# RWKV of batch 0 and the state-space constants placed in the last attention's final slots, late weights loaded there

## The chip, the cores and the metric

The kernel runs on one NeuronCore of a Trainium2 chip. The metric is the device time in microseconds (us) of the whole program, the median of several runs. Engines are called by their names in the profile: PE (TensorE), ACT (ScalarE), DVE (VectorE), POOL (GpSimd), SP (SyncE, which only issues DMAs here). Each has an instruction stream of its own, executed in order; they meet at semaphores.

## The reference, cut to what matters

The input is x, 8 batches of 512 tokens by 128 channels. Eight residual steps follow, each of the form x + layer(layernorm(x)):

```python
x = x + _L2_attn_ref(_layernorm(x), W_qkv)              # full attention, 16 heads of 8
x = x + _L2_ffn_ref(_layernorm(x), W_r, W_k, W_v, mu_r, mu_k)
x = x + _L3_attn_ref(_layernorm(x), W_in, conv_w, conv_b, W_x, B_log, W_out, ln_g, ln_b)
x = x + _L3_ffn_ref(_layernorm(x), ...)                 # experts

# _L2_ffn_ref, the RWKV channel mix
xr = mu_r * x + (1.0 - mu_r) * x_prev
xk = mu_k * x + (1.0 - mu_k) * x_prev
r = sigmoid(xr @ W_r.T)
out = r * (square(relu(xk @ W_k.T)) @ W_v.T)
```

The four steps before these are a block-masked attention, an FP4 FFN, an ALiBi attention and a ternary FFN. `_L3_attn_ref` is a state-space layer: projection, short convolution, silu, a scan with decay 0.95, a product with C times exp(B_log), a gate, an output projection and a layernorm of its own. The product of W_x's C part with exp(B_log) doesn't depend on x; it is one 256x256 matrix, `couple`.

## The kernel before, in words

X stays in SBUF throughout, 128 partitions by 8 x 512 columns, one 512-column stretch per batch. There are six stages: attention, FP4 FFN, attention, ternary FFN, attention (`l2`, kind "full"), and `Tail`, which runs the RWKV layer (`RwkvFfn`), the state-space layer (`Ssm`) and the experts (`ExpertFfn`) as a pipeline of batches. A stage starts on each engine with `stage_starts`: wait until the stage before has written X of batch 7 (`s_x_done`).

**The attention's order.** `frames` runs a body for c from -1 to 8, and each frame has 16 slots (`slots`). In frame c the slots 0 to 7 hold key groups 8 to 15 of batch c-1, the slots 8 to 15 groups 0 to 7 of batch c; the row maxima of the next batch are computed beside them. In the last frame (c = 8) only groups 8 to 15 of batch 7 are left, in slots 0 to 7, and no maxima. A slot on PE: two score heads (`head_t`, L398 or L386 in the trace), half of the previous group's product with V (`half_pv`, L412, 8 matmuls), two more heads, the other half. ACT does four `exp` per slot (L593). PSUM banks 0 to 2 hold scores, 3 to 5 the scores for the maxima, 6 the product with V, 7 the rest. After each quarter ACT copies bank 6 (L606), PE transposes it (`context_t`, through `transpose4`, L2878), DVE divides it (L749, L751), and after the fourth quarter POOL adds it to X (L899). The attention takes a `guest`: after every slot each engine calls the guest's `early_*`. In this kernel only the first attention has one (the FP4 stage).

**The normalised batch 0 of the tail** is made in the attention's frame 7 already (`norm_stats`, `norm_apply` for batch `c + 1 = 8`, which `norm_of` turns into batch 0 of the next stage).

**The tail's order.** `Tail.frames` runs c from -3 to 7. Frame c works on the experts of batch c, opens the experts of c+1, runs the state-space layer of c+2 and RWKV of c+3. So frame -3 has nothing but RWKV of batch 0, and at its end (`opening`) the state-space constants: `exp(B_log)` on ACT (L1855), the product on PE (L1814), its copy into `couple` (L1857). Frame -2 begins on PE with the transposes of the state-space layer's batch 0 (`Ssm.pe_turn`) and holds the folding of the expert weights (`folding`).

RWKV of one batch: turn (PE, L2878), two scaled copies (ACT, L1709), mix (DVE, L1731), keys (PE, L1688), relu (ACT, L1714), square (POOL, L1742), receptance (PE, L1693), sigmoid (ACT, L1719), values (PE, L1701), product (DVE, L1737), add to X (POOL, L1747). Then comes the state-space norm: statistics (DVE, L1626, L1631), `Norm.apply` (POOL, L1638 to L1647) and `pool_shift` (POOL, L1945).

**The late weights** are 27 transfers (`load_late`, L2807), issued by SP at the stage's start, because they go into `Qst`, `V` and `Kst`, which the attention uses until its end. The first 8 of them are the state-space layer's and count on `s_late`, the other 19 on `s_later`. POOL waits at the start of its tail stream for all 19 (`e.k.wait_late(pool)`), ahead of `pool_square`.

`Qst`, `V` and `Kst` have a half for even and one for odd batches.

Of the kernel before, what the change touches and what calls it, by code (L numbers as in the profile page):

```python
# [20 lines left out]
NB = 8  # L21
# [1630 lines left out]
class RwkvFfn:  # L1652

    def __init__(self, k, st, bank, tile):
        def s(name, per):
            return k.started(f"rwkv_{name}", per)

        self.k, self.bank = k, bank  # L1660
# [73 lines left out]
    def dve_product(self, dve, n):  # L1734
        dve.wait_ge(self.s_v_ps.sem, self.s_v_ps.at(n))
        dve.wait_ge(self.s_x_done.sem, self.s_x_done.at(n.plus(-1)))
        dve.tensor_tensor(self.prod, self.bank, self.r, ALU.mult).then_inc(self.s_prod.sem, 1)  # L1737
# [5 lines left out]

    def pool_add(self, pool, n):
        pool.wait_ge(self.s_prod.sem, self.s_prod.at(n))
        x = xs_of(self.k.X, n)
        pool.tensor_tensor(x, x, self.prod, ALU.add).then_inc(self.s_x_done.sem, 1)  # L1747


class Ssm:  # L1750
# [6 lines left out]
    def __init__(self, k, before, banks, old, tile):  # L1757
# [36 lines left out]
        self.loads = len(k.late_loads)  # L1794
        self.expb = k.late([self.STATE, self.D_IN])
        self.couple = k.late([P, self.MT, self.D_IN])
        self.decay = k.sb("decay", [P, 1])
# [11 lines left out]

    def pe_constants(self, pe):  # L1810
        self.loaded(pe)
        pe.wait_ge(self.s_expb, 1)
        for kt in range(self.MT):
            mm = pe.matmul(self.banks[0][:, self.D_IN * kt:self.D_IN * (kt + 1)], self.wx[:, P * kt:P * kt + P],  # L1814
                           self.expb[:, :], start=True, stop=True)
        mm.then_inc(self.s_couple_ps, 1)
        pe.wait_ge(self.s_couple, 1)

# [33 lines left out]

    def act_constants(self, act):
        self.loaded(act)
        act.activation(self.expb[:, :], self.blog[:, :], ACT.Exp).then_inc(self.s_expb, 1)  # L1855
        act.wait_ge(self.s_couple_ps, 1)
        act.activation(self.couple[:, :, :].rearrange("p a b -> p (a b)"), self.banks[0], ACT.Copy)\  # L1857
           .then_inc(self.s_couple, 1)
# [26 lines left out]

    def dve_stats(self, dve, n):
        dve.wait_ge(self.before.sem, self.before.at(n))
        self.norm.stats(dve, n)
# [404 lines left out]
class Tail(Stage):  # L2293
# [5 lines left out]

    def __init__(self, k, stage, fp4, ternary):  # L2300
        self.fp4, self.ternary = fp4, ternary
        super().__init__(k, stage)

    def prepare(self, k):
# [6 lines left out]
        ps = [k.ps[:, j, :] for j in range(8)]  # L2311
        self.rwkv = RwkvFfn(k, self, ps[5], tile)
        self.ssm = Ssm(k, self.s_x_done, ps[6:8], self.fp4.q_x, tile)
# [3 lines left out]
    def frames(self, body):  # L2317
        for c in range(-3, NB):
            body(N(None, c), c == -3, c == -2)

    def tensor(self, pe):
# [3 lines left out]

        def frame(f, opening, folding):
            before, en, sn, rn = f.plus(-1), f.plus(1), f.plus(2), f.plus(3)
            for j in range(e.STEPS):
# [52 lines left out]
                elif j == 7:  # L2381
                    if sn.valid():
                        s.pe_out(pe, sn)
            if opening:
                s.pe_constants(pe)

        self.frames(frame)
        end = N(None, NB - 1)
# [4 lines left out]
    def scalar(self, act):  # L2393
        self.k.stage_starts(act, self)
        r, s, e = self.rwkv, self.ssm, self.expert

        def frame(f, opening, folding):
            before, en, sn, rn = f.plus(-1), f.plus(1), f.plus(2), f.plus(3)
            for j in range(e.STEPS):
# [40 lines left out]
                elif j == 7:  # L2440
                    if en.valid():
                        e.act_exp(act, en)
            if opening:
                s.act_constants(act)

# [3 lines left out]
    def vector(self, dve):  # L2449
        self.k.stage_starts(dve, self)  # L2450
        r, s, e = self.rwkv, self.ssm, self.expert
        r.dve_constants(dve)
        s.dve_constants(dve)

        def frame(f, opening, folding):
            before, en, sn, rn = f.plus(-1), f.plus(1), f.plus(2), f.plus(3)
            for j in range(e.STEPS):
# [53 lines left out]
    def gpsimd(self, pool):  # L2511
        self.k.stage_starts(pool, self)
        r, s, e = self.rwkv, self.ssm, self.expert
        e.k.wait_late(pool)

        def frame(f, opening, folding):
            en, sn, rn = f.plus(1), f.plus(2), f.plus(3)
# [6 lines left out]
            if rn.valid():  # L2524
                r.pool_add(pool, rn)
# [56 lines left out]
def make_stages(k):  # L2582
# [13 lines left out]
    fp4, ternary = Fp4Ffn(k, 1), TernaryFfn(k, 3)  # L2596
    fp4.after, ternary.after = l1, l2
    l0.guest, fp4.before = fp4, l0
    return [l0, fp4, l1, ternary, l2, Tail(k, 5, fp4, ternary)]

# [76 lines left out]
class Kernel:  # L2677


    def __init__(self, nc, ctx, dram, out):  # L2680
# [63 lines left out]

        self.late_mem = [self.Qst[:, :, :, :].rearrange("p a h t -> p (a h t)").bitcast(F32),
                         self.V[:, :, :, :, :].rearrange("p a t h e -> p (a t h e)"),
                         self.Kst[:, :, :, :].rearrange("p a h t -> p (a h t)").bitcast(F32)]
        self.late_at = [0, 0, 0]
        self.s_late = self.sem("late_weights")
# [30 lines left out]
    def late(self, shape, src=None, dt=F32):  # L2780

        size = int(np.prod(shape[1:])) * mybir.dt.size(dt) // 4
        r = next(r for r in range(3) if self.late_at[r] + size <= self.late_mem[r].shape[1])
        at = self.late_at[r]
# [171 lines left out]
def transformer(nc, dram, out):  # L2956
    with ExitStack() as ctx:
# [7 lines left out]
        def _(sp):  # L2965
# [76 lines left out]
```

## Time and profile before

| | us |
|---|---|
| median of 3 runs | 2067.47 |
| lowest, highest | 2064.45, 2068.32 |
| the profiled execution | 2065.46 |
| its span, first to last instruction | 2063.6 |
| PE busy | 1811.4 (88%) |
| DVE busy | 1298.7 (63%) |
| ACT busy | 1043.0 (51%) |
| POOL busy | 709.3 (34%) |

Times in the rows are us from the span's start. The last attention runs from about 1288 to 1654, the tail from there to the end. Only the join of the two is touched. A row of a timeline gives start, length, engine, line, operation, the tiles written and read, and how many instructions are merged; the bracket behind it is the engine's idle time before it and what ended that. PE's ends are modelled, and neighbours overlap: the distance of two starts tells more than the length.

### The profile page before, as it was taken

The page shows a single profiled execution, that of the slowest core. Times are in us where ns is not written, and L with a number is a line of the kernel's source. Part 1 is how long each engine was busy: PE and PEld are TensorE (multiplying, and loading weights), DVE is VectorE, ACT ScalarE, POOL GpSimd, SP SyncE. Part 2 cuts the span into 40 slices and gives each one's busy share as a digit, 9 for nine tenths or more (in the row PEclk, how much of TensorE's full clock was granted, in tenths as well). Part 3 has the DMA queues.
Part 4 walks back from the last instruction along what each step waited for, and adds up shares of the span by engine and source line. Part 5 has one row for each costly group of instructions (what it writes and reads, how often), then busy time and mean ns, then how long its engine had stood idle before and what let it go on. Part 6 is the DMA issues. An engine that isn't in the chain of part 4 may idle for free.

```text
span 2063.6 us, 33125 instructions
## 1 busy us (share of the span) xinstructions
PE 1811.4 (88%) x11885; PEld 815.9 (40%) x11885; DVE 1298.7 (63%) x3442; ACT 1043.0 (51%) x1768; POOL 709.3 (34%) x796
## 2 busy tenths in 40 slices
PE   4898888667669999988999999999999958999998
PEld 1233333234434444444445443333223234444443
DVE  3777777469867877761101114999899546666663
ACT  1566666522216666653322321888888834444432
POOL 4376676545522233201111102222223036444420
PEclk9899999777859999998999997999999978999999
DMA  6354222000033224400000020333222010000000
GB/s 132 98 140 95 63 63 63 1 17 1 0 101 85 63 63 103 84 2 3 0 0 1 0 57 6 98 81 70 63 63 63 2 51 1 6 6 6 6 11 11
DMA packets 67963, 91.68 MB, mean 44 GB/s; under 512 B 10924, under 2 KB 61340, under 8 KB 62924
## 3 DMA queue, kind: packets, MB, share of 16 engines
q1 hardware_dynamic: 66072, 89.04, 18.0%
q8 instruction: 95, 1.56, 0.3%
q10 hardware_dynamic: 1728, 0.53, 0.2%
q14 instruction: 68, 0.56, 0.1%
HBM read 49.30 MB, written 39.85 MB: 43 GB/s over the span
## 4 chain that ended last, share of the span: by engine, by line
PE 55%; issue 6%; DVE 4%; ACT 4%; DMA 2%; SPq 1%; POOL 1%; DVEq 0%; ACTq 0%; POOLq 0%
PE ps L1435 5%; PE ps L412 5%; PE ps L1447 5%; PE ps L2878 4%; PE ps L386 3%; PE ps L1412 3%; PE ps L370 3%; PE ps L2148 3%; PE ps L398 3%; PE ps L2150 2%; PE ps L2166 2%; PE ps L354 2%; PE ps L332 2%; DMA Qst<-mT 2%; ACT Pr L593 2%
## 5 line engine op out<-in xcount | busy, mean ns | idle before, releaser
L702 DVE TENSOR_REDUCE mx<-ps 128x1 f32<-128x512 f32 (+3 forms) x1024 | 534.3, 583 | 111.1 <-PE ps L354 82.6
L600 ACT ACTIVATE Pr<-ps 128x1024 f32<-128x1024 f32 (+3 forms) x512 | 348.0, 707 | 184.7 <-PE ps L337 95.9
L593 ACT ACTIVATE Pr<-ps 128x512 f32<-128x512 f32 x512 | 275.4, 601 | 44.9 <-PE ps L386 38.1
L354 PE MATMUL ps<-Kst,Qst 63*128 63x512 bf16 (+3 forms) x1024 | 223.2, 317 | 57.3 <-DVE mx L702 29.2
L698 DVE CUSTOM_DVE_ANT_0 vs<-ps,cT 128x512 f32<-128x512 f32 (+3 forms) x512 | 225.9, 488 | 63.2 <-PE ps L354 59.9
L332 PE MATMUL ps<-Qst,Kst 64*128 64x512 bf16 (+3 forms) x1024 | 223.4, 312 | 20.0 <-ACT Pr L600 8.3
L2906 POOL TENSOR_TENSOR ve<-mv,eps 128x4 f32<-128x4 f32 x41 | 8.3, 201 | 591.6 <-DVE mv L2895 591.6
L370 PE MATMUL ps<-Pr,V 128*32 128x512 f32 (+3 forms) x2048 | 198.4, 460 | 6.4 <-ACT ctxU L606 2.9
L398 PE MATMUL ps<-Kst,Qst 63*128 63x512 bf16 x512 | 172.5, 403 | 5.5 <-DVE mx L702 3.3
L412 PE MATMUL ps<-Pr,V 128*32 128x256 f32 x2048 | 164.6, 394 | 8.6 <-ACT ctxU L606 7.7
L386 PE MATMUL ps<-Qst,Kst 64*128 64x512 bf16 x512 | 157.2, 387 | 10.1 <-DMA Qst<-mT 5.8
L354 PEld LDWEIGHTS ps<-Kst,Qst 63*128 63x128 bf16 x1024 | 68.9, 95 | 194.4 <-DVE mx L702 99.4
L332 PEld LDWEIGHTS ps<-Qst,Kst 64*128 64x128 bf16 x1024 | 71.7, 94 | 121.2 <-ACT Pr L600 64.1
L1447 PE MATMUL ps<-f_shared,w_L_h2T 128*128 128x512 f32 x256 | 115.1, 592 | 0.0
L1435 PE MATMUL ps<-f_shared,w_L_h1T 128*128 128x512 f32 x256 | 112.8, 593 | 0.7 <-ACT xT L1523 0.7
L1580 DVE SCALAR_TENSOR_TENSOR f_shared<-ps,w_L_s_w,f_own 128x512 f32<-128x512 f32 x32 | 24.0, 750 | 122.6 <-PE ps L1412 118.1
L1562 DVE TENSOR_TENSOR ctxU<-ps,w_L_s_w 128x512 f32<-128x512 f32 x8 | 5.5, 692 | 151.4 <-PE ps L1424 151.4
L848 POOL TENSOR_TENSOR rec<-dn,mone 128x16 f32<-128x16 f32 x32 | 93.0, 2907 | 0.0
L337 PE MATMUL ps<-tri_kq,ident_h 64*128 64x128 bf16 x512 | 85.2, 220 | 0.0
L335 PE MATMUL ps<-tri_kq,ident_h 64*128 64x128 bf16 x512 | 85.1, 220 | 0.0
L412 PEld LDWEIGHTS ps<-Pr,V 128*32 128x32 f32 x2048 | 40.7, 108 | 95.6 <-issue 73.3
L386 PEld LDWEIGHTS ps<-Qst,Kst 64*128 64x128 bf16 x512 | 32.9, 94 | 113.5 <-ACT Pr L593 75.9
(340 smaller groups left out, 3277.9 us busy)
## 6 DMA issues: line engine op xcount, KB each, us to landing
Qst<-parts_scratch SPq DMA_DIRECT2D x48, 384.0 KB, 6.3
Kst<-parts_scratch SPq DMA_DIRECT2D x48, 384.0 KB, 8.4
parts_scratch<-qpart SPq DMA_DIRECT2D x24, 384.0 KB, 2.7
parts_scratch<-kpart SPq DMA_DIRECT2D x24, 384.0 KB, 3.3
parts_scratch<-qpart SPq DMA_DIRECT2D x24, 256.0 KB, 2.9
parts_scratch<-kpart SPq DMA_DIRECT2D x24, 256.0 KB, 3.3
parts_scratch<-qpart SPq DMA_DIRECT2D x24, 128.0 KB, 2.8
parts_scratch<-kpart SPq DMA_DIRECT2D x24, 128.0 KB, 3.3
```

Of the source, the lines that this page charges most:

```text
L332: mm = pe.matmul(out, k.Kst[rows, b.par, 2 * q + tile, P * jt:P * jt + P], k.Qst[rows, b.par, 2 * q + tile, T - W:T], start=True, stop=not ...
L354: mm = pe.matmul(ps[:, 4 + a, lo:lo + W], k.Qst[rows, n.par, pair, P * it:P * it + P], k.Kst[rows, n.par, pair, 0:W], start=True, stop=True)
L370: mm = pe.matmul(ps[32 * a:32 * a + 32, 6, lo:hi], k.V[:, b.par, jt, 4 * q + a, :], k.Pr[:, g % 2, a, lo - (T - W):hi - (T - W)], start=jt ...
L386: pe.matmul(ps[:, self.bank_t(b, g, j), :], k.Kst[rows, b.par, 2 * q + tile, P * jt:P * jt + P], k.Qst[rows, b.par, 2 * q + tile, :], star ...
L398: pe.matmul(ps[:, self.bank_m(n, u), :], k.Qst[rows, n.par, pair, P * it:P * it + P], k.Kst[rows, n.par, pair, :], start=True, stop=True). ...
L412: mm = pe.matmul(ps[32 * a:32 * a + 32, 6, lo:hi], k.V[:, b.par, jt, 4 * q + a, :], k.Pr[:, g % 2, a, lo:hi], start=jt == 0 and half == 0, ...
L593: act.activation(k.Pr[:, g % 2, 2 * (j // 2) + 1 - j % 2, :], ps[:, self.bank_t(b, g, j), :], ACT.Exp).then_inc(self.s_exp.sem, 1)
L600: act.activation(k.Pr[:, g % 2, 2 * tile:2 * tile + 2, 0:W], ps[:, 2 * tile:2 * tile + 2, 0:W], ACT.Exp).then_inc(self.s_exp.sem, 1)
L698: dve.tensor_tensor_reduce(k.vs[:, at_u % 2, T - W:T], ps[:, bank, lo:lo + W], k.cT[:, 1, T - W:T], 1.0, -3e38, ALU.add, ALU.max, k.mx[:, ...
L702: dve.tensor_reduce(k.mx[:, half, at:at + 1], ps[:, bank, lo:lo + W], AX_X, ALU.max, negate=True).then_inc(self.s_max.sem, 1)
L1435: mm = pe.matmul(ps[:, at + m, :], self.h1[:, kt, P * m:P * m + P], self.hidden[0][:, kt, :], start=kt == 0, stop=kt == self.KT - 1)
L1447: mm = pe.matmul(ps[:, at + m, :], self.h2[:, kt, P * m:P * m + P], self.hidden[1][:, kt, :], start=kt == 0, stop=kt == self.KT - 1)
```

## The change

`Tail` becomes the guest of the last attention, and its frame -3 is gone. What frame -3 did is spread over the attention's last frame (c = 8), behind the given slots: turn and the two scaled copies behind slot 0, mix behind 1, keys and relu behind 2, receptance behind 3, the gate r behind 4, values and product behind 6, the constants' `exp` behind 6, their product on PE behind 7 and its copy behind 8. The gate is no longer ACT's sigmoid: ACT does `exp(-x)`, DVE adds 1 and takes the reciprocal. POOL does `Norm.apply` of batch 1, square, add, `Norm.apply` of the state-space layer and `pool_shift`, all ahead of its last `X + ctx`. DVE does the statistics for the state-space norm of batch 0 ahead of the division of the last quarter.

The late weights all go to the even halves of `Qst`, `V` and `Kst`, which no batch uses after batch 6, and SP issues them after its last attention transfer, once batch 6 is done. Work areas of the experts go to the odd halves first; `expb` and `couple` move into `qpart`. POOL's wait for the 19 transfers moves behind the work of frame -2.

```diff
     def frames(self, body):
-        for c in range(-3, NB):
-            body(N(None, c), c == -3, c == -2)
+        for c in range(-2, NB):
+            body(N(None, c), c == -2)
+    def early_tensor(self, pe, f, s):
+        if f.c != NB:
+            return
+        r, zero = self.rwkv, N(None, 0)
+        if s == 0:
+            pe.wait_ge(self.before.s_max.sem, self.before.s_max.at(f.plus(-1)))
+            r.pe_turn(pe, zero)
+        elif s == 2:
+            r.pe_keys(pe, zero)
+        elif s == 3:
+            r.pe_receptance(pe, zero)
+        elif s == 6:
+            r.pe_values(pe, zero)
+        elif s == 7:
+            self.ssm.pe_constants(pe, self.k.ps[:, 4, :])
+
+    def early_scalar(self, act, f, s):
...
+        if s == 0:
+            r.act_first(act, zero)
+        elif s == 2:
+            r.act_relu(act, zero)
+        elif s == 4:
+            r.act_exponential(act, zero)
+        elif s == 6:
+            act.wait_ge(self.before.s_q_out.sem, self.before.s_q_out.at(f.plus(-1)))
+            self.ssm.act_exponential(act)
+        elif s == 8:
+            self.ssm.act_couple(act, self.k.ps[:, 4, :])
+
+    def early_vector(self, dve, f, s):
...
+        if s == 0:
+            r.dve_constants(dve)
+            self.ssm.dve_constants(dve)
+            r.norm.stats(dve, one)
+        elif s == 1:
+            r.dve_mix(dve, zero)
+        elif s == 4:
+            r.dve_inverse(dve, zero)
+        elif s == 6:
+            r.dve_product(dve, zero)
+        elif s == 8:
+            self.ssm.dve_stats(dve, zero, r.s_added)
+
+    def early_gpsimd(self, pool, f, point):
...
+        if point == 0:
+            r.norm.apply(pool, N(None, 1), r.s_xnT_ps)
+        elif point == 1:
+            r.pool_square(pool, zero)
+        elif point == 2:
+            r.pool_add(pool, zero, r.s_added)
+        elif point == 3:
+            ssm.norm.apply(pool, zero, ssm.s_res)
+            ssm.loaded(pool)
+            ssm.pool_shift(pool, zero)
...
+    def act_exponential(self, act, n):
+        act.wait_ge(self.s_r_ps.sem, self.s_r_ps.at(n))
+        act.activation(self.r, self.bank, ACT.Exp, scale=-1.0).then_inc(self.s_denominator.sem, 1)
+
+    def dve_inverse(self, dve, n):
+        dve.wait_ge(self.s_denominator.sem, self.s_denominator.at(n, 1))
+        dve.tensor_scalar(self.r, self.r, 1.0, None, ALU.add).then_inc(self.s_denominator.sem, 1)
+        dve.wait_ge(self.s_denominator.sem, self.s_denominator.at(n, 2))
+        dve.reciprocal(self.r, self.r).then_inc(self.s_r.sem, 1)
...
-        e.k.wait_late(pool)
-
-        def frame(f, opening, folding):
+        pool.memset(e.k.mone[:, :], -1.0).then_inc(r.s_x_done.sem, 1)
+
+        def frame(f, folding):
...
             if en.valid():
+                if en.c == 0:
+                    e.k.wait_late(pool)
                 e.pool_centre(pool, en)
...
                 if st.stage == max(FIRST_STAGE, FIRST_LATE):
-                    k.stage_starts(sp, st)
+                    attention, n = st.before, N(None, NB - 2)
+                    sp.wait_ge(attention.s_scores.sem, attention.s_scores.at(n))
+                    sp.wait_ge(attention.s_scores_t.sem, attention.s_scores_t.at(n))
+                    sp.wait_ge(attention.s_pv.sem, attention.s_pv.at(n))
                     k.load_late(sp, st.ssm.loads)
```

## Rows read from the trace of the kernel before

**Rows 1.** Windows: us, then each engine's busy us (and instructions), PE clock, DMA

```profile
1620.00:1640.00 20.00, 18.46 (x179) 5.98 (x176) 6.52 (x14) 17.83 (x37) 0.00 (x0) 1.00 0.01 1
1660.00:1680.00 20.00, 6.12 (x20) 4.73 (x20) 3.08 (x17) 4.48 (x6) 8.40 (x10) 0.50 0.34 97
```

**Rows 2.** The chain that ended last, at the join: start, us, what

```profile
1652.62 1.27 POOL X L899
1653.90 0.36 SPq L2807
...
1667.32 2.52 DMA V<-in_c_select
1670.05 1.05 POOL f_shared L1742
...
1680.34 1.94 PE ps L2878 x8
```

**Rows 3.** Timeline of SP's queue: its last transfers of the attention

```profile
1607.28 21.80 SPq L946 DMA_DIRECT2D Qst<-mT  x4
```

**Rows 4.** Timeline of PE: a part of a slot of the last frame, its end

```profile
1635.39 0.39 PE L386 MATMUL ps<-Qst,Kst 64*128 64x512 bf16 x2
1635.71 0.64 PE L412 MATMUL ps<-Pr,V 128*32 128x256 f32 x8
1636.28 0.57 PE L386 MATMUL ps<-Qst,Kst 64*128 64x512 bf16 x2
...
1649.41 1.07 PE L412 MATMUL ps<-Pr,V 128*32 128x256 f32 x16 [0.60 <-ACT Pr L593]
1651.29 0.63 PE L2878 MATMUL ps<-ident,ctxU 128*128 128x128 f32 x4 [0.81 <-ACT ctxU L606]
```

**Rows 5.** Timeline of ACT: last frame, then frame -3 of the tail

```profile
1632.66 0.63 ACT L606 ACTIVATE ctxU<-ps 128x512 f32<-128x512 f32 x1
...
1635.81 6.33 ACT L593 ACTIVATE Pr<-ps 128x512 f32<-128x512 f32 x12 [0.39 <-PE ps L386]
...
1655.35 0.68 ACT L1709 ACTIVATE f_shared<-ps,w_L_mu_k 128x512 f32<-128x512 f32 x1
1659.70 0.60 ACT L1714 ACTIVATE f_shared<-ps 128x512 f32<-128x512 f32 x1 [3.67 <-PE ps L1688]
1660.32 1.28 ACT L1719 ACT_TABLE_LOAD   x1
...
1664.37 0.42 ACT L1855 ACTIVATE Qst<-Qst 16x256 f32<-16x256 f32 x1
```

**Rows 6.** Timeline of PE: constants of frame -3, keys and receptance of frame -2

```profile
1673.21 2.07 PE L1814 MATMUL ps<-Qst 16*128 16x256 f32 x4
...
1686.67 1.02 PE L1688 MATMUL ps<-f_shared,w_L_WkfT 128*128 128x512 f32 x2
...
1689.69 1.05 PE L1693 MATMUL ps<-w_L_WrT,f_shared 128*128 128x128 f32 x8
```

**Rows 7.** DVE groups by shape: count, busy us, mean ns, idle before

```profile
L1023 DVE RECIPROCAL fq_h_inv<-fq_h_over 128x88 f32<-128x88 f32 x8 | 5.6, 703 | 0.3
...
L1028 DVE TENSOR_SCALAR f_shared<-f_shared 128x512 f32<-128x512 f32 x8 | 3.5, 440 | 0.3
...
L1023 DVE RECIPROCAL fq_x_inv<-fq_x_over 128x32 f32<-128x32 f32 x8 | 2.8, 353 | 0.3
```

**Rows 8.** Timeline of DVE: mix, product and statistics in frame -3

```profile
1656.13 1.41 DVE L1731 SCALAR_TENSOR_TENSOR f_shared<-ps,one_minus_mu,f_shared 128x511 f32<-128x511 f32 x2 [0.80 <-ACT f_shared L1709]
1673.32 0.69 DVE L1737 TENSOR_TENSOR f_shared<-ps,f_shared 128x512 f32<-128x512 f32 x1 [15.78 <-PE ps L1701]
1675.59 0.87 DVE L1626 BATCH_NORM_STATS2 ssm_bn<-X 128x6 f32<-128x128 f32 x4 [1.58 <-POOL X L1747]
```

**Rows 9.** Timeline of POOL: add, start of the state-space norm, shift

```profile
1674.29 1.26 POOL L1747 TENSOR_TENSOR X<-X,f_shared 128x512 f32<-128x512 f32 x1
1676.95 0.20 POOL L1638 TENSOR_TENSOR ssm_ve<-ssm_mv,eps 128x4 f32<-128x4 f32 x1 [1.40 <-DVE ssm_mv L1631]
...
1680.20 1.09 POOL L1945 TENSOR_TENSOR X<-X,Qst 128x512 f32<-128x512 f32 x1
```

More of the change, by code:

```diff
@@ L1652, with __init__ @@
 class RwkvFfn:
-    def __init__(self, k, st, bank, tile):
+    def __init__(self, k, st, bank, old, tile):
         def s(name, per):
             return k.started(f"rwkv_{name}", per)
+        self.s_denominator = Signal(old.s_magic.sem, 2, 0, old.s_magic.start + 2)
+        self.s_added = Signal(old.s_rounded.sem, 1, 0, old.s_rounded.start + 1)
         self.k, self.bank = k, bank
@@ L1742, in pool_square, with pool_add @@
         pool.tensor_tensor(self.act, self.relu, self.relu, ALU.mult).then_inc(self.s_act.sem, 1)
-    def pool_add(self, pool, n):
+    def pool_add(self, pool, n, done):
         pool.wait_ge(self.s_prod.sem, self.s_prod.at(n))
         x = xs_of(self.k.X, n)
-        pool.tensor_tensor(x, x, self.prod, ALU.add).then_inc(self.s_x_done.sem, 1)
+        pool.tensor_tensor(x, x, self.prod, ALU.add).then_inc(done.sem, 1)
 class Ssm:
@@ L1794, in __init__ @@
         self.loads = len(k.late_loads)
-        self.expb = k.late([self.STATE, self.D_IN])
-        self.couple = k.late([P, self.MT, self.D_IN])
+        flat = k.qpart[:, :, :].rearrange("p a t -> p (a t)").bitcast(F32)
+        self.expb = flat[0:self.STATE, 0:self.D_IN]
+        self.couple = flat[:, self.D_IN:3 * self.D_IN].rearrange("p (a b) -> p a b", a=self.MT)
         self.decay = k.sb("decay", [P, 1])
@@ L1808, in loaded, with pe_constants @@
         eng.wait_ge(self.k.s_late, 16 * self.loads)
-    def pe_constants(self, pe):
+    def pe_constants(self, pe, bank):
         self.loaded(pe)
@@ L1851, in pe_out, with act_exponential, act_couple @@
         mm.then_inc(self.s_out_ps.sem, 1)
-    def act_constants(self, act):
+    def act_exponential(self, act):
         self.loaded(act)
         act.activation(self.expb[:, :], self.blog[:, :], ACT.Exp).then_inc(self.s_expb, 1)
+    def act_couple(self, act, bank):
         act.wait_ge(self.s_couple_ps, 1)
-        act.activation(self.couple[:, :, :].rearrange("p a b -> p (a b)"), self.banks[0], ACT.Copy)\
+        act.activation(self.couple[:, :, :].rearrange("p a b -> p (a b)"), bank, ACT.Copy)\
            .then_inc(self.s_couple, 1)
@@ L1884, in dve_constants, with dve_stats @@
         dve.memset(self.decay[:, :], self.DECAY).then_inc(self.s_decay, 1)
-    def dve_stats(self, dve, n):
-        dve.wait_ge(self.before.sem, self.before.at(n))
+    def dve_stats(self, dve, n, added):
+        dve.wait_ge(added.sem, added.at(n))
         self.norm.stats(dve, n)
@@ L2293, with __init__ @@
 class Tail(Stage):
-    def __init__(self, k, stage, fp4, ternary):
-        self.fp4, self.ternary = fp4, ternary
+    def __init__(self, k, stage, fp4, ternary, before):
+        self.fp4, self.ternary, self.before = fp4, ternary, before
         super().__init__(k, stage)
@@ L2395, in scalar, with frame @@
         r, s, e = self.rwkv, self.ssm, self.expert
-        def frame(f, opening, folding):
+        def frame(f, folding):
             before, en, sn, rn = f.plus(-1), f.plus(1), f.plus(2), f.plus(3)
@@ L2451, in vector, with frame @@
         r, s, e = self.rwkv, self.ssm, self.expert
-        r.dve_constants(dve)
-        s.dve_constants(dve)
-        def frame(f, opening, folding):
+        def frame(f, folding):
             before, en, sn, rn = f.plus(-1), f.plus(1), f.plus(2), f.plus(3)
@@ L2524, in frame @@
             if rn.valid():
-                r.pool_add(pool, rn)
+                r.pool_add(pool, rn, r.s_x_done)
                 s.norm.apply(pool, rn, s.s_res)
@@ L2597, in make_stages @@
     fp4.after, ternary.after = l1, l2
+    tail = Tail(k, 5, fp4, ternary, l2)
     l0.guest, fp4.before = fp4, l0
-    return [l0, fp4, l1, ternary, l2, Tail(k, 5, fp4, ternary)]
+    l2.guest = tail
+    return [l0, fp4, l1, ternary, l2, tail]
 def layout(inp):
@@ L2743, in __init__ @@
         self.late_loads = []
[L2745 to L2748, printed above, removed]
+        stacks = "p h t -> p (h t)"
+        self.late_mem = [m for a in range(2) for m in (
+            self.Qst[:, a].rearrange(stacks).bitcast(F32), self.V[:, a].rearrange("p t h e -> p (t h e)"),
+            self.Kst[:, a].rearrange(stacks).bitcast(F32))]
+        self.late_at = [0] * 6
         self.s_late = self.sem("late_weights")
@@ L2782, in late @@
         size = int(np.prod(shape[1:])) * mybir.dt.size(dt) // 4
-        r = next(r for r in range(3) if self.late_at[r] + size <= self.late_mem[r].shape[1])
+        order = (3, 4, 5, 0, 1, 2) if src is None else (0, 1, 2)
+        r = next(r for r in order if self.late_at[r] + size <= self.late_mem[r].shape[1])
         at = self.late_at[r]
```

26 lines of the change are left out of this document (16 added, 10 removed).

## The prediction

> **What bounds the kernel now.** Begin with the windows: in the last frame of the attention, 1620 to 1640, ACT is busy 17.83 of 20 us and PE 18.46; in 1660 to 1680 no engine is busy more than 8.40, and PE works 6.12 us at a granted clock of 0.50, its lower level of 1.2 GHz [rows 1]. That hole is what the change aims at. Then the chain at the join: it runs from POOL's last add of the attention (ends 1653.89) into SP, which issues the first late transfer at 1653.90 and the last of 27 at 1667.32 (one each 0.5 us); that one lands 2.52 us later, and only then POOL squares (1670.05), because it waited for all of them. Behind it come values, constants and copy, and POOL's norm, until PE starts frame -2 at 1680.34 [rows 2]. So the join costs 1680.34 - 1653.89 = 26.45 us. From 1680.34 on I expect the same work in the same order, so the question is when frame -2 starts afterwards: call it T. The gain is 1680.34 - T.
>
> **The transfers.** SP's four mT transfers end at 1629.08 [rows 3]; the conditions on batch 6 are older. So the loads run from about 1629.1 to 1629.1 + (1667.32 - 1653.90) + 2.52 = 1645.0 [rows 2]. The first eight (8 x 0.5 + 2.5) are there by 1636. ACT wants them behind slot 6, near 1650, POOL for the shift near 1657, frame -2 for all of them after that. They are hidden with 5 to 14 us to spare and cost nothing; if this cover were gone, every microsecond past 1650 would come on T. The mT transfers are issued before them.
>
> **The slots: what ACT and PE must do in addition.** Both are nearly full there. ACT needs 6.33 / 3 = 2.11 us per slot for its four exps [rows 5]. PE needs 0.32 for two heads and 0.57 for half a product (distances of starts), twice, 1.78 [rows 4]; 0.3 us per slot is free. Into this go, on ACT, two scaled copies (2 x 0.68, overlapped 1.2), relu 0.60, exp(-x) 0.60 and the constants' exp 0.42 [rows 5], 2.8 in all. PE gets turn 0.63 [rows 4], keys 1.02 and receptance 1.05 at full clock, values like receptance, overlapped 0.9 to 1.0 each, and the constants at half of the 2.07 they took at clock 0.50 [rows 6], 4.4 in all. Bound below 2.8 (ACT alone), above 2.8 + 4.4 + 1.4 for the mix = 8.6 (nothing overlaps). I walk through the slots, with 0.42 from the start of a head to the exp that reads it:
> - Slot 0: PE turns at 1632.3, while it would wait for the copy of bank 6 (1632.66 to 1633.29 [rows 5]), so free. ACT's two copies follow, the exps of slot 1 start at 1634.3, 1.2 late.
> - Slots 1, 2: the context transposes move to 1636.5, DVE divides, then mixes for 1.41 [rows 8] until 1638.55. Keys wait for it and run 1638.6 to 1639.5, behind them the heads of slot 3. ACT relu at 1639.65; exps of slot 3 at 1640.15, 2.2 late.
> - Slot 3: receptance 1641.65 to 1642.55, heads after it; exps of slot 4 at 1642.95, 3.0 late.
> - Slot 4: copy of bank 6, exp(-x) until E = 1646.0; exps of slot 5 at 1645.9, 3.4 late. Slot 6's exps start at 1648.35, 3.2 late.
> - Slot 6: values 1649.9 to 1650.8, constants' exp beside them; exps of slot 7 at 1651.2, 3.9 late.
> - Slot 7 and 8: constants 1652.7 to 1653.7, the last two half products to 1654.8 instead of 1650.48 [rows 4], 4.3 late. Copy, context transposes, division: context ready at 1656.75.
>
> **The gate r.** Reciprocal was never run at 512 columns here. 32 took 353 ns and 88 took 703 [rows 7], so 6.25 ns a column and 153 fixed: 3.35 us at 512. Add 1 takes the 440 ns of the tensor_scalar of 128x512 [rows 7]. r is ready at 1646.0 + 0.45 + 3.35 + 0.1 = 1649.9, the moment PE gets to the values anyway (1649.85); bounds: 0 on T if it were faster, and a microsecond on T for each it is slower. DVE is idle then but for the third quarter's division, which waits behind the reciprocal until 1650.5; nobody needs that before the fourth quarter's transposes at 1655. The table load of 1.28 that sigmoid brought [rows 5] isn't there; relu came without one [rows 5], exp is the attention's.
>
> The Trainium skill ("VectorE: DVE Perf Modes", section "Walkthrough: the 8-slice pipeline in each mode") says that reciprocal is an iterated divide with a repeat count of 8, and its clock is given as 0.96 GHz. Read as 8 cycles a column that is an estimate of 8.3 ns, 4.3 us at 512, and T would be 0.9 later. The rows' slope of 6.25 ns disagrees with that reading, and I keep the rows.
>
> **POOL's and DVE's queues then set T.** After the values (end V = 1650.8) nothing is parallel: product 0.69 [rows 8], add to X 1.26 [rows 9], statistics 0.87 and aggregation, 1676.95 - 1675.59 = 1.36 with the handover [rows 8, 9], state-space norm and shift 1676.95 to 1681.29 = 4.34 [rows 9], and POOL's last add for batch 7, 1.27 [rows 2], which stands behind all of that in POOL's order although its context is ready at 1656.75. With 0.1 of handovers, 9.05 us: T = 1650.8 + 9.05 = 1659.9. The add that ends the attention thus waits 1.9 us (1658.6 instead of 1656.75) for POOL: that is a new wait, and the stage start on all engines is queued behind it. Batch 1's norm on POOL, as long as the state-space norm, runs before slot 1 in the idle time, DVE's statistics for it too; couple is copied by 1656. PE is idle from 1656.2 to T, so frame -2 starts at the lower clock, as it did at 1680.34 (window before it 0.50 [rows 1]): no difference. DVE's statistics of batch 2 (1.3 us), once done early in frame -3, now start at T; the mix of batch 1 has to wait for PE's two turns and ACT's two copies first, over 2 us, so they stay hidden.
>
> Sum: 1680.34 - 1659.9 = 20.4 us off the profiled execution's 2065.46, 2045.1. The runs' median is 2.0 above that execution, and the same gain gives 2067.47 - 20.4 = **2047.1**.
>
> **Rivals.**
> (1) The slots overlap better than I walked: T set by ACT's 2.8 alone, V at 1648.5, T at 1657.5, 2044.7. For it: PE's lengths are modelled. Against: keys wait for the mix, values for r. Chance 0.10.
> (2) The slots don't overlap: last product 8.6 late instead of 4.3, values and all behind them 4.3 later, T = 1664.2, 2051.4. For it: ACT and PE form one loop, and every new step is one engine waiting for another. Against: PE turns and multiplies in waits it has today. Chance 0.14.
> (3) The change doesn't do what it says for the loads: they are late. SP's queue or a wait on batch 6 holds them until the attention ends near 1654.8; the first eight land at 1661.5 instead of before 1650.3, and T moves with ACT's exp by 11: 2058. Against: SP stood idle from 1629.08 to 1653.90 [rows 2, 3]. Chance 0.02.
> (4) Slower than before, by the clock. The new waits of PE in the slots (0.4 to 0.6 us for mix and r) make the chip take PE to 1.2 GHz in the last frame. Were that so from slot 0 on, the eight slots would take 8 x 2 x 1.78 = 28.5 us, the added 4.4 would be 8.8, the last product, copy and transposes 3.5, and what stands behind in DVE's and POOL's order (statistics are early now) some 7: T = 1630.3 + 28.5 + 8.8 + 3.5 + 7 = 1678. It decides from T = 1680.34 on, that is if 20.4 us are lost; another 4 us in frame -2, whose matmuls at half clock take twice as long as the 1.02 and 1.05 of [rows 6], carry it there: about 2069. Against: with the guest's work PE is busy over 90% of the window, and the clock was 1.00 there with a wait of 0.60 [rows 1, 4]; it was 0.50 where PE stood free for whole stretches. Chance 0.03.
>
> The skill's rule behind (4) ("TensorE: Matmul & The Clock Gate", section "HAM oscillation — how this bites in real kernels") is that idle gaps of the array between bursts of matmuls take its clock down. The trace bears it out for the long hole of frame -3 and not for gaps of 0.6 us.
>
> **The numbers.** The forecast 2047.1 has 0.71 and is good to about 3 us (a handover more or less in each of nine steps, the runs' own spread of 3.9). The range takes in (1) and (2) at their values and leaves out (3), (4) and the outer side of (2): 2042 to 2053. About 0.2%, 4.1 us, is what a measurement of this kernel can tell from no change. Faster by more than that are the forecast and (1) to (3), 0.97; I keep 0.02 of it for what the profile doesn't show: faster 0.95, within it 0.02, slower 0.03.
>
> **What would show it.** Right: late transfers from 1629 to 1645; POOL without a wait on them; a reciprocal of 3.35 us on DVE; PE's last L412 ending near 1655; POOL's last add starting straight after its shift, near 1658.6; the first transposes of frame -2 at about 1660, and from there on the same distances as from 1680.34 before. Wrong: PE's clock under 1.00 between 1630 and 1655, slots over 3 us on average, a wait of ACT on `s_late`, or frame -2 longer than before.

## The result and the profile after

The changed kernel took 2044.74 us in the median of 4 runs (2042.05 to 2047.69), the kernel before 2065.96 in the same series (2062.72 to 2068.32): a ratio of 0.991, 95% interval 0.9891 to 0.9929. The forecast was 2047.1, a gain of 20.4; the medians give 21.2. Two more series, below, gave 0.9919 (0.9904 to 0.9934) and 0.9894 (0.9874 to 0.9915). The profiled execution took 2045.97, its span is 2044.2.

In this execution everything ahead of the change ran 2.38 us earlier: the last frame starts (first L386 behind the mT transfer) at 1627.93 instead of 1630.31. That start lies anywhere from 1624.97 to 1628.36 in the three traces of the full change and from 1627.31 to 1630.31 in the three of the kernel before, so a part of it at least is the spread of executions. In what follows times are counted from that row, and T is the start of frame -2, the first transposes of `Ssm.pe_turn`. The row of before, and the two of after:

```profile
1630.31 0.39 PE L386 MATMUL ps<-Qst,Kst 64*128 64x512 bf16 x2 [0.66 <-DMA Qst<-mT]
```

```profile
1627.93 0.39 PE L386 MATMUL ps<-Qst,Kst 64*128 64x512 bf16 x2 [0.66 <-DMA Qst<-mT]
...
1658.10 1.11 PE L2961 MATMUL ps<-ident,f_shared 128*128 128x128 f32 x4 [3.63 <-POOL X L899]
```

The windows of after, with the columns of [rows 1]. The hole at 1660 to 1680 is gone, PE works 18.02 there:

```profile
1620.00:1640.00 20.00, 18.39 (x165) 6.49 (x163) 6.74 (x23) 17.21 (x35) 4.25 (x5) 1.00 0.43 125
1640.00:1660.00 20.00, 14.95 (x129) 7.21 (x127) 7.92 (x23) 11.08 (x22) 6.84 (x8) 0.93 0.04 8
1660.00:1680.00 20.00, 18.02 (x66) 10.49 (x66) 13.11 (x31) 11.25 (x17) 6.47 (x8) 0.84 0.01 1
```

The chain at the join, which in [rows 2] ran through SP and a transfer, now runs through the values, DVE's product, POOL's add, DVE's statistics and POOL's queue (state-space norm, shift, last add):

```profile
1647.92 1.10 PE ps L1704 x8
...
1649.05 0.70 DVE f_shared L1751
...
1649.82 1.28 POOL X L1761
...
1655.73 1.09 POOL X L1961
1656.83 1.23 POOL X L899
1658.05 0.04 issue
1658.10 1.97 PE ps L2961 x8
```

SP's queue, where [rows 3] end with the mT transfers: the late weights follow at once, 27 of them, the last issued at 1639.49. No engine waits for them.

```profile
1625.57 1.14 SPq L946 DMA_DIRECT2D Qst<-mT  x2
1626.81 0.51 SPq L2890 DMA_DIRECT2D Qst<-in_L_WinT  x1
...
1639.49 0.43 SPq L2890 DMA_DIRECT2D Kst<-in_c_select  x1
```

PE in the slots, against [rows 4] and [rows 6]: keys, receptance, values and constants stand between heads (L386) and products with V (L412), at full clock; the last product ends at 1653.03:

```profile
1636.13 1.12 PE L1691 MATMUL ps<-f_shared,w_L_WkfT 128*128 128x512 f32 x2
1637.19 0.39 PE L386 MATMUL ps<-Qst,Kst 64*128 64x512 bf16 x2
...
1639.32 1.16 PE L1696 MATMUL ps<-w_L_WrT,f_shared 128*128 128x128 f32 x8
1640.41 0.39 PE L386 MATMUL ps<-Qst,Kst 64*128 64x512 bf16 x2
...
1647.29 0.64 PE L412 MATMUL ps<-Pr,V 128*32 128x256 f32 x8
1647.86 1.16 PE L1704 MATMUL ps<-w_L_WvfT,f_shared 128*128 128x128 f32 x8
1648.95 0.39 PE L386 MATMUL ps<-Qst,Kst 64*128 64x512 bf16 x2
...
1651.96 1.07 PE L412 MATMUL ps<-Pr,V 128*32 128x256 f32 x16
```

ACT, against [rows 5], at slot 4: no table load between the exps; and DVE, against [rows 7], the gate:

```profile
1642.75 0.63 ACT L606 ACTIVATE ctxU<-ps 128x512 f32<-128x512 f32 x1
1643.23 0.65 ACT L1726 ACTIVATE f_shared<-ps 128x512 f32<-128x512 f32 x1
1643.71 2.13 ACT L593 ACTIVATE Pr<-ps 128x512 f32<-128x512 f32 x4
```

```profile
1643.91 0.43 DVE L1730 TENSOR_SCALAR f_shared<-f_shared 128x512 f32<-128x512 f32 x1 [7.83 <-ACT f_shared L1726]
1644.37 3.35 DVE L1732 RECIPROCAL f_shared<-f_shared 128x512 f32<-128x512 f32 x1
```

From the last frame's start to T: 1680.34 - 1630.31 = 50.03 us before, 1658.10 - 1627.93 = 30.17 after, a gain of 19.86. But from T to the end of the span it is 383.26 before and 386.10 after, 2.84 us given back: frame -2 took 30.69 instead of 25.92, 4.77 longer, and frame -1 was 1.96 shorter. That the spans still differ by 19.4 is owed to the 2.38 us ahead of the change.

The 4.77 us can be placed. In frame -2 of before the coupling is

```profile
1697.47 3.67 PE L1841 MATMUL ps<-f_own,Qst 128*128 128x512 f32 x8 [1.99 <-issue]
```

and in after the coupling and the output projection are

```profile
1676.83 5.37 PE L1855 MATMUL ps<-f_own,qpart 128*128 128x512 f32 x8 [1.98 <-issue]
1685.21 3.78 PE L1863 MATMUL ps<-Qst,Pr 128*128 128x128 f32 x16 [3.02 <-DVE Pr L1933]
```

Counted from T, the coupling starts 1.60 us later than before (18.73 against 17.13) and the projection 4.26 later (27.11 against 22.85, its start at 1703.19); its own length brings the other 0.5. So two questions were open: whether the 20 us come from where I said, and whether the change lengthens frame -2.

### The profile page after: what moved, and what is told of

The parts are those of the page before. It is cut to its first block, busy times and chain, and to the rows that moved or that the text cites. A ratio compares the mean times of both kernels' runs of the same rounds, so it can differ in the third digit from the quotient of the medians.

```text
span 2044.2 us, 33125 instructions
## 1 busy us (share of the span) xinstructions
PE 1806.4 (88%) x11885; PEld 812.6 (40%) x11885; DVE 1301.7 (64%) x3444; ACT 1038.4 (51%) x1766; POOL 709.2 (35%) x797
## 4 chain that ended last, share of the span: by engine, by line
PE 55%; issue 6%; DVE 4%; ACT 3%; DMA 2%; POOL 1%; SPq 0%; DVEq 0%; ACTq 0%; POOLq 0%
PE ps L1435 5%; PE ps L412 5%; PE ps L1447 5%; PE ps L386 4%; PE ps L2961 3%; PE ps L1412 3%; PE ps L2164 3%; PE ps L370 3%; PE ps L398 3%; PE ps L2182 2%; PE ps L2166 2%; PE ps L354 2%; PE ps L332 2%; DMA Qst<-mT 2%; PE ps L1855 1%
## 5 line engine op out<-in xcount | busy, mean ns | idle before, releaser
L332 PE MATMUL ps<-Qst,Kst 64*128 64x512 bf16 (+3 forms) x1024 | 222.9, 311 | 19.6 <-ACT Pr L600 8.2
L412 PE MATMUL ps<-Pr,V 128*32 128x256 f32 x2048 | 163.8, 392 | 7.4 <-ACT ctxU L606 7.3
L386 PE MATMUL ps<-Qst,Kst 64*128 64x512 bf16 x512 | 157.5, 385 | 11.4 <-DMA Qst<-mT 6.5
L386 PEld LDWEIGHTS ps<-Qst,Kst 64*128 64x128 bf16 x512 | 33.0, 94 | 114.4 <-ACT Pr L593 75.1
L1518 ACT ACTIVATE f_own<-ps,w_L_s_w 128x512 f32<-128x512 f32 x32 | 22.0, 687 | 110.1 <-PE ps L1412 109.0
```

Source lines behind the costliest of these rows:

```text
L332: mm = pe.matmul(out, k.Kst[rows, b.par, 2 * q + tile, P * jt:P * jt + P], k.Qst[rows, b.par, 2 * q + tile, T - W:T], start=True, stop=not ...
L386: pe.matmul(ps[:, self.bank_t(b, g, j), :], k.Kst[rows, b.par, 2 * q + tile, P * jt:P * jt + P], k.Qst[rows, b.par, 2 * q + tile, :], star ...
L412: mm = pe.matmul(ps[32 * a:32 * a + 32, 6, lo:hi], k.V[:, b.par, jt, 4 * q + a, :], k.Pr[:, g % 2, a, lo:hi], start=jt == 0 and half == 0, ...
```

## The experiments

One table for all traces; "join" is last frame's start to T, "-2" and "-1" the lengths of these frames from first transposes to first transposes, "rest" from T to the end of the span.

| kernel | join | -2 | -1 | -2 and -1 | rest |
|---|---|---|---|---|---|
| before | 50.03 | 25.92 | 34.65 | 60.57 | 383.3 |
| before_again | 49.92 | 25.92 | 34.83 | 60.75 | 383.5 |
| before_third | 48.75 | 28.43 | 34.15 | 62.58 | 385.2 |
| after | 30.17 | 30.69 | 32.69 | 63.38 | 386.1 |
| after_again | 30.17 | 26.07 | 34.75 | 60.82 | 383.6 |
| after_third | 30.17 | 28.55 | 34.13 | 62.68 | 385.4 |
| loads_only | 41.74 | 27.97 | 33.91 | 61.88 | 384.6 |
| sigmoid | 34.34 | 30.45 | 32.70 | 63.15 | 385.8 |
| no_reciprocal | 30.17 | 30.34 | 32.69 | 63.03 | 385.7 |
| shift_behind | 29.12 | 27.75 | 33.87 | 61.62 | 383.8 |
| warm | 30.17 | 23.87 | 35.04 | 58.91 | 381.6 |
| fold_wait_later | 30.16 | 27.88 | 32.60 | 60.48 | 382.7 |
| all_three | 29.13 | 25.48 | 32.68 | 58.16 | 380.4 |
| warm_twice | 29.13 | 23.80 | 33.58 | 57.38 | 379.6 |

From frame 0 on the distances from frame to frame are the same in all of them, 43.3 and then 43.7, and what lies behind frame -1 is 322.2 or 322.7 us. With the change the join repeats to 0.01 us in kernels that issue the same work there; in the kernel before, where it waits for a transfer, it went from 48.75 to 50.03. The runs of one and the same kernel spread over 3 to 14 us. Differences of a few microseconds are therefore read from the join, not from medians.

**Does frame -2 get longer: before_again, after_again, after_third, before_third.** No edit.

> The kernel before once more, for the spread of its trace. Start of the last frame (first L386 behind the mT transfer) to first transposes of frame -2: 50.0 us as in the first trace, within 0.5, by both theories. Length of frame -2 (its first transposes to those of frame -1), 25.9 in the first trace. Theory A (the 4.8 us that frame -2 is longer in the trace of after, 30.7, come from where the low-clock stretches of PE fall in one execution, not from the change): another value here, anywhere between 25.5 and 31. Rival B (the change makes frame -2 longer, because PE stands idle for 3.6 us right before it): 25.9 within 0.5 again.

before_again: one run, 2063.70 us; join 49.92, frame -2 25.92 once more, which is what rival B said.

> The changed kernel once more, timed. Both theories: start of the last frame to frame -2 30.2 us within 0.5; 19 to 22 us faster than before by the runs. Frame -2, 30.7 in its first trace: theory A (where the low clock falls is chance) gives a value anywhere between 25.5 and 31, rival B (the change makes it longer) 30.7 within 0.5.

after_again: 2047.36 in the median of 6 runs against 2063.68, 16.3 us faster and not the 19 to 22 expected, although the join is the same 30.17. Frame -2 took 26.07, which rules out rival B's 30.7 for this kernel. The granted clock on PE at its start tells the two executions of the same kernel apart; first after, T = 1658.10, then after_again, T = 1655.14 (window, PE busy, clock, DMA):

```profile
1658.00:1660.00 2.00, 1.90 (x8) 0.50 0.00 0
1660.00:1662.00 2.00, 2.00 (x4) 0.50 0.04 8
1662.00:1664.00 2.00, 2.00 (x5) 0.50 0.00 0
1664.00:1666.00 2.00, 2.00 (x8) 0.97 0.00 0
```

```profile
1655.00:1657.00 2.00, 1.86 (x8) 0.50 0.00 0
1657.00:1659.00 2.00, 2.00 (x4) 0.66 0.03 8
1659.00:1661.00 2.00, 2.00 (x9) 1.00 0.00 0
```

In the one the clock came back 6 us after T, in the other after 3. In the first the clock was also low behind the stop of 2 us ahead of the coupling (L1855): its matmuls took 5.37 us, and 3.67 in after_again.

> The full change a third time, beside the next kernel on the same chip. Theory A: start of the last frame to frame -2 30.17 within 0.1; frames -2 and -1 together one of the values seen, 60.8 to 63.4, by where the low clock falls.

after_third: 2043.27 against 2063.83; join 30.17, frames -2 and -1 62.68, between the two.

> The kernel before a third time. Frame -2 took 25.9 us in both of its traces (frames -2 and -1 together 60.6 and 60.8), in the full change 30.7, 26.1 and 28.6 (63.4, 60.8 and 62.7). Theory A (where the low clock falls is chance in both kernels): both sums in the same band, so this one anywhere from 60.5 to 63.4. Rival (the kernel before always has the short case, the change gives back 1 to 2 us on average): 60.6 within 0.3 again. Start of the last frame to frame -2 50.0.

before_third: one run, 2063.16 us; frame -2 28.43, with 62.58 for both frames, so the kernel before has a longer case too, and the rival's 60.6 within 0.3 is out. Theory A holds so far: each kernel spreads by 2 us or more from execution to execution. That the change costs nothing here on average isn't shown.

The lengths of frame -2 fall into three cases, by two rows. In the short case (25.9 to 26.1) the coupling takes 3.67 us and the output projection 3.2 to 3.3. In the two others the coupling takes 5.37, and the projection 2.05 in the middle one (27.8 to 28.6: before_third, after_third, loads_only, shift_behind) and 3.78 in the long one (30.3 to 30.7). The long one was seen in after, sigmoid and no_reciprocal alone, never in a kernel without the change. Three traces of before and of after (60.6, 60.8, 62.6 against 63.4, 60.8, 62.7) have means of 61.3 and 62.3 over both frames; so a cost of 1 us or somewhat more on average stays open.

In before_third the join was 48.75 instead of 50: SP issued one of its transfers (W_invT) in 0.43 us, which had taken 1.41 and 1.33, and the last landed in 2.13 instead of 2.52. That too differs from execution to execution, and it is on the path of the kernel before alone.

**What each part is worth: loads_only.**

```diff
-        self.late_mem = [self.Qst[:, :, :, :].rearrange("p a h t -> p (a h t)").bitcast(F32),
...
+        stacks = "p h t -> p (h t)"
+        self.late_mem = [m for a in range(2) for m in (
+            self.Qst[:, a].rearrange(stacks).bitcast(F32), self.V[:, a].rearrange("p t h e -> p (t h e)"),
+            self.Kst[:, a].rearrange(stacks).bitcast(F32))]
...
-                    k.stage_starts(sp, st)
+                    attention, n = st.before, N(None, NB - 2)
...
+                    sp.wait_ge(attention.s_pv.sem, attention.s_pv.at(n))
```

> Only the transfers of the change: late weights in the even halves and issued in the attention's last frame; frame -3 stays in the tail, with sigmoid. Theory A (both parts carry the gain): POOL squares right behind relu, 9.7 us earlier than before, then values, product, add, statistics and norm follow; frame -2 starts 41.7 us behind the start of the last frame instead of 50.0, so 8.3 us faster than before, 11.5 slower than the full change. Rival (the hole was the transfers alone, the slots give back what frame -3 cost): 17 us or more faster than before, within 3 us of the full change.

2055.85 us in the median of 5 runs against 2063.68, ratio 0.9961 (0.9948 to 0.9974); join 41.74 where 41.7 was expected. POOL no longer waits for transfers but for relu:

```profile
1658.75 1.04 POOL L1742 TENSOR_TENSOR f_shared<-f_shared 128x512 f32<-128x512 f32 x1 [6.68 <-ACT f_shared L1714]
...
1664.19 1.26 POOL L1747 TENSOR_TENSOR X<-X,f_shared 128x512 f32<-128x512 f32 x1 [1.15 <-DVE f_shared L1737]
```

Of the 19.9 us of the join 8.3 are the transfers' (7.0 if before_third's join is taken) and 11.6 the slots'. The slots without the early transfers weren't tried: the constants placed there need them.

**Whether the gate sets it: sigmoid and no_reciprocal.** sigmoid computes the gate as before, with ACT's sigmoid:

```diff
         elif s == 4:
-            r.act_exponential(act, zero)
+            r.act_sigmoid(act, zero)
...
-        elif s == 4:
-            r.dve_inverse(dve, zero)
```

> The full change, but the gate r by ACT's sigmoid behind slot 4, as the kernel before computes it, without DVE's add and reciprocal. Theory A (ACT's time counts in full, DVE's 3.8 us are hidden behind slots 5 and 6): two table loads of 1.28 us each stand in ACT's stream, exps of slot 5 2.6 us later, values and frame -2 2.6 later: start of the last frame to frame -2 32.8 instead of 30.2, 2.6 us slower than the full change. Rival (the gate r is what values wait for, so r 2 us earlier is worth it): within 0.7 us of the full change or faster.

Join 34.34, 4.17 more than the full change and not 2.6. The direction is theory A's, the size isn't. ACT has the two loads, 2.57 us in all. They also end the overlap of neighbouring ACT instructions, so that the exps of slot 5 start 2.89 us later than in after, counted from the last frame's start (18.67 against 15.78). PE stands still behind them for 2.86:

```profile
1641.79 1.28 ACT L1722 ACT_TABLE_LOAD   x1
1643.08 0.60 ACT L1722 ACTIVATE f_shared<-ps 128x512 f32<-128x512 f32 x1
1643.70 1.28 ACT L593 ACT_TABLE_LOAD   x1
```

```profile
1645.65 0.59 PE L386 MATMUL ps<-Qst,Kst 64*128 64x512 bf16 x1 [2.86 <-ACT Pr L593]
1646.17 1.08 PE L412 MATMUL ps<-Pr,V 128*32 128x256 f32 x8
1647.18 1.11 PE L2959 MATMUL ps<-ident,ctxU 128*128 128x128 f32 x4
```

The product with V takes 1.08 instead of 0.64 and the transposes 1.11 instead of 0.66: after that stop PE works at its lower level, granted clock 0.50, for some 3 us. By the exps of slot 6 the delay is 4.16, so the low clock is the other 1.3. This is the mechanism of rival 4 of the prediction, in small. In the medians nothing of it is seen: 2047.21 against 2047.36 of after_again, with runs from 2039.41 to 2053.19; the medians alone would have called the sigmoid harmless.

no_reciprocal leaves the reciprocal out, so r is 1 + exp(-x) and the kernel computes something else; it serves for the timing only:

```diff
         dve.wait_ge(self.s_denominator.sem, self.s_denominator.at(n, 1))
-        dve.tensor_scalar(self.r, self.r, 1.0, None, ALU.add).then_inc(self.s_denominator.sem, 1)
-        dve.wait_ge(self.s_denominator.sem, self.s_denominator.at(n, 2))
-        dve.reciprocal(self.r, self.r).then_inc(self.s_r.sem, 1)
+        dve.tensor_scalar(self.r, self.r, 1.0, None, ALU.add).then_inc(self.s_r.sem, 1)
```

> The full change without DVE's reciprocal: r = 1 + exp(-x) goes into the product for batch 0 as it is (only for the timing). Theory A (the reciprocal's 3.35 us end 0.15 us before PE gets to the values, PE's own order sets them): start of the last frame to frame -2 30.17 within 0.2. Rival (r is what the values wait for, the equal times are no accident): up to 3.3 us less, under 29.

Join 30.17, the same to 0.01 (one run, 2045.64). The reciprocal is hidden, if only just: in after, PE gets to the values at 1647.86, and r is ready 0.14 us earlier (1644.37 + 3.35 = 1647.72).

**Whether POOL's queue sets it: shift_behind.**

```diff
         elif point == 3:
             ssm.norm.apply(pool, zero, ssm.s_res)
-            ssm.loaded(pool)
-            ssm.pool_shift(pool, zero)
...
         pool.memset(e.k.mone[:, :], -1.0).then_inc(r.s_x_done.sem, 1)
+        s.loaded(pool)
+        s.pool_shift(pool, N(None, 0))
```

> The full change, with the state-space bias shift of batch 0 taken out of POOL's stream ahead of the attention's last add and put at the start of its tail stream. Theory A (frame -2 starts when POOL has worked off its queue: add, norm, shift, last add): the shift's 1.05 us go, start of the last frame to frame -2 29.1 instead of 30.2. Rival (the last context sets it, ready at the same time as the norm): unchanged at 30.2.

Join 29.12: 1.05 us less, the shift's whole time. Ratio 0.9889 (0.9858 to 0.992), 4 runs; after_third has 0.9894, so the medians don't show the microsecond. POOL:

```profile
1656.38 1.04 POOL L1647 TENSOR_TENSOR f_shared<-f_own,ssm_rstd 128x512 f32<-128x512 f32 x1
1657.37 1.26 POOL L899 TENSOR_TENSOR X<-X,ctx 128x512 f32<-128x512 f32 x1
1658.69 0.10 POOL L2589 MEMSET mone<- 128x1 f32 x1
1658.75 1.09 POOL L1961 TENSOR_TENSOR X<-X,Qst 128x512 f32<-128x512 f32 x1
```

**What the low clock costs: warm.** 24 transposes of the identity, into bank 0, whose result nobody reads.

```diff
     def tensor(self, pe):
+        for t in range(24):
+            pe.transpose(self.k.ps[:, 0, 0:P], self.k.ident[:, :], self.k.ident[:, :])
         self.k.stage_starts(pe, self)
```

> The full change, with 24 transposes on PE that nobody reads, into a free PSUM bank, in the 3.6 us in which PE waits for frame -2. Theory A (what frame -2 gives back is the low clock at its start and in its later waits): start of the last frame to frame -2 unchanged at 30.2 within 0.3, PE clock 1.00 at its start, frame -2 24.3 us instead of 26.1 and 30.7. Rival (ACT and DVE bound frame -2, PE's clock matters only when it falls later): 25.9 within 0.4.

Join 30.17, clock 1.00 through the join and the whole of frame -2, which took 23.87 (24.3 was expected), against 25.9 to 30.7 in all traces without these transposes. PE at the join; the turn takes 0.66 instead of 1.11 and `pe_inner` 1.98 instead of 3.78:

```profile
1656.65 2.78 PE L2405 MATMUL ps<-ident 128*128 128x128 f32 x24
1660.44 0.66 PE L2963 MATMUL ps<-ident,f_shared 128*128 128x128 f32 x4 [1.01 <-POOL X L899]
1660.93 0.60 PE L2963 MATMUL ps<-ident,xn 128*128 128x128 f32 x4
1661.92 1.98 PE L1842 MATMUL ps<-Pr,Qst 128*128 128x512 f32 x4 [0.39 <-ACT Pr L1879]
```

So against the full change the low clock in frame -2 is worth 2.2 us in the short case (26.07 - 23.87) and up to 6.8 in the long one. Frame -1 took 35.04, the longest of all: a part moves on, and over both frames the gain is 1.9 to 4.5 us. This is one trace; the ratio, 0.9899 (0.9871 to 0.9927) in 4 runs, can't be told from that of the full change.

**PE's stop ahead of the coupling: fold_wait_later.**

```diff
             mm(self.XV, self.bT, self.woT).then_inc(self.s_fold_ps, 1)
-            self.folded(pe)
...
+            if f.c == -1:
+                e.folded(pe)
```

> The full change, with PE's wait for the split bias of the experts moved from the middle of frame -2 (ahead of the state-space coupling) to the start of frame -1. Theory A (PE's stop of 2 us there isn't on the path by itself, since DVE's scan ends as late; it only lets the clock fall): the stop is gone, coupling isn't at half clock, frame -2 25.8 to 26.5. Rival (the stop is on the path): frame -2 2 us shorter than the shortest so far, 24 or less. Chance alone (the stop has no part in it): somewhere between 26 and 30.7.

27.88: theory A's 25.8 to 26.5 missed, and inside the 26 to 30.7 that chance alone allowed. The stop of 1.98 us went, the coupling ran at full clock (as in after_again, which has the stop), and PE then stood still for 3.99 us ahead of the output projection, which waits for DVE's gated product. Behind this longer stop the clock was low:

```profile
1672.94 3.70 PE L1855 MATMUL ps<-f_own,qpart 128*128 128x512 f32 x8
1680.63 3.78 PE L1863 MATMUL ps<-Qst,Pr 128*128 128x128 f32 x16 [3.99 <-DVE Pr L1933]
```

I had looked at whether the stop is on the path and not at the stop that its time would be added to. That it isn't on the path the later runs show: with the clock at 1.00 up to there, the projection starts 21.98 us into frame -2 with the stop (warm) and 21.91 without it (all_three). The ratio is 0.9893 (0.9865 to 0.9921), 4 runs, no different from the full change.

**Together: all_three and warm_twice.** all_three has the edits of shift_behind, warm (16 transposes) and fold_wait_later.

> The full change with three edits together: the shift of batch 0 behind the attention's last add, 16 unread transposes on PE while it waits for frame -2, PE's wait for the split bias at the start of frame -1. Theory A: start of the last frame to frame -2 29.1 instead of 30.17; PE clock 1.00 at its start; frame -2 23.8 us or a little less, frames -2 and -1 together under 59.5; in all 2.5 to 5 us faster than the full change. Rival (the low clock only moves on, the later frames take back what frame -2 gains): frames -2 and -1 together 60.5 or more, 1 us faster by the shift alone.

2039.33 us in the median of 6 runs, against 2043.27 of after_third and 2063.83 of before on the same chip; ratio to before 0.9874 (0.9855 to 0.9894). Their intervals overlap, so the 3.9 us between the medians of all_three and after_third rest on the traces. Join 29.13, frames -2 and -1 58.16, as expected; frame -2 alone is 25.48 and not 23.8: behind the stop of 3.99 us, which is there again, the projection takes 3.78 us.

warm_twice fills that stop too:

```diff
                 elif j == 7:
+                    if folding:
+                        e.folded(pe)
+                        for t in range(28):
+                            pe.transpose(e.WB[:, 0:P], self.k.ident[:, :], self.k.ident[:, :])
```

> As all_three, and 28 more unread transposes on PE in frame -2, behind the coupling, while PE waits 3.99 us for DVE's gated product. Theory A (that product comes 21.9 us after the start of frame -2 whatever PE does; the stop costs only by the low clock behind it): start of the last frame to frame -2 29.1; output projection starts 21.9 us into frame -2 and takes 2.05 us instead of 3.78; frame -2 23.8 instead of 25.48, frames -2 and -1 together 58.2 less 1.7, or up to 58.5 where the low clock moves into frame -1. Rival (the clock falls by chance whatever PE does in these 4 us): 25.5 or more for frame -2 again.

```profile
1672.94 3.22 PE L2468 MATMUL ps<-ident 128*128 128x128 f32 x28
1677.09 2.05 PE L1863 MATMUL ps<-Qst,Pr 128*128 128x128 f32 x16 [0.94 <-DVE Pr L1933]
```

The projection starts 1677.09 - 1655.18 = 21.91 us into frame -2, as it did in warm (21.98) and in all_three (21.91), and takes 2.05; frame -2 23.80 instead of 25.48, frame -1 33.58 instead of 32.68, so that 0.8 us are left over both frames (57.38). Ratio 0.9874 (0.9852 to 0.9895), median 2037.64 of 5 runs: the ratio is all_three's. This is the shortest kernel by the trace, 29.13 + 379.6 = 408.7 us from the last frame's start to the end; the three traces of the full change have 413.8, 415.6 and 416.3, 5.0 to 7.5 more.

## Why the prediction was right

The transfers: hidden as said. The last is issued 1639.49 - 1627.93 = 11.6 us after the last frame's start; 12.2 was implied (1642.5 - 1630.3). loads_only shows their share.

The slots: the walk held. Counted from the last frame's start, exps of slot 1 3.96 (walked 3.99), keys 8.20 (8.3), exps of slot 3 9.86 (9.84), receptance 11.39 (11.34), exps of slot 4 12.90 (12.64), of slot 5 15.78 (15.6), values 19.93 (19.6), exps of slot 7 21.44 (20.9), end of the last product 25.10 (24.5), T 30.17 (29.6). The 0.6 us are one term that was too small: each float32 step of PE in the slots. From the starts above, keys block PE for 1.06, receptance and values for 1.09, constants for 1.05, where the walk had 0.9, 0.9, 0.9 and 1.0. It had taken the overlapped part of the rows of frame -2 (0.86 between two starts there), but heads behind such a step don't overlap with it that way. Rivals 1 and 2 (T at 1657.5 or 1664.2, that is a join of 27.2 or 33.9) are both excluded by the join of 30.17.

The gate: 3.35 us for the reciprocal, read from two short ones, was measured as 3.35, and not as the 4.3 that the prediction set against it; no_reciprocal shows that it costs nothing.

POOL's queue: from the end of the values (1649.02) to T 9.08 us, forecast 9.05. The new wait of the last add was said to be 1.9 us; it was 1.69 (context ready at 1655.09, add at 1656.78), and shift_behind took 1.05 of it away.

Rival 3: no wait on the transfers. Rival 4: the clock was 1.00 from the last frame's start to PE's last transposes there, with waits of PE up to 0.68 in the slots and 0.81 behind them. What sigmoid showed is that a single wait of 2.86 us there had the low clock behind it.

What didn't hold is the sentence that from frame -2 on everything keeps its distances. "Frame -2 longer than before" was among the prediction's own signs of being wrong, and the first trace showed it. The lower clock at its start was seen, and its length taken from one execution: 3 us there, 3 to 6 in others. The step is "frame -2 starts at the lower clock, as it did: no difference". From T to the end it was 383.3 to 386.1 us in six traces of the two kernels, a spread of 2.8, where the whole join was off by 0.6; it belonged into the range as a term of its own. The range 2042 to 2053 held, but the 3 us beside the forecast had been put down to handovers, which differ by hundredths, and to the runs' spread. That the first profiled execution came out 0.9 us from the 2045.1 of the sum is in part luck: 0.6 in the join and 2.8 behind T were lost, and 2.4 ahead of the last frame, where no work was moved, came back.

## What to carry to other kernels

A stage's lonely first batch can go into the last frame of the stage before even where both its engines look full: the price is the sum of what the two add in turn (4.9 us here, and POOL's queue behind), and it saved 11.6 us of a hole of 26. Work that is issued ahead of an engine's last step of a stage holds up the whole next stage, so order that queue by who waits, not by batch. And when a stop of PE that isn't on the path is removed, look at the next stop: its time is added there (1.98 us gone, 3.99 instead of 2.04 to 3.02), and the clock can be low behind that one. Whether two short stops are cheaper than one long one isn't shown here.

## What the runs showed of the hardware

The length of a low-clock stretch isn't a property of the kernel. The same program, with the same rows up to T, got the full clock back 3 us after T in one execution and 6 in another, and over frames -2 and -1 that made 2.6 us. The stop of 1.98 us ahead of the coupling had the clock at 1.00 behind it in after_again and warm (3.67 us for the coupling) and 0.50 in after and shift_behind (5.37 and 5.35). Stops of 2.58 (shift_behind, ahead of T), 2.86 (sigmoid), 3.63 (after, ahead of T) and 3.99 us (fold_wait_later) each had the lower level behind them. Transposes that nobody reads kept it up: 24 of them, 2.78 us of PE, and frame -2 was 2.2 us shorter than in the shortest trace of the full change.

Reciprocal on DVE at 128x512 takes 3354 ns, 7.9 times the 426 ns of adding 1 to the same tile.

SP's issue of one transfer took 1.41, 1.33 and 0.43 us in three executions of the kernel before, most of the others 0.43 each.
